# Two mixture stages that gather their expert rows by a list in place of scattering them

## The reference

```python
# first mixture (L0), z = layernorm(x)
gates = softmax(z @ gate_w); topw, topi = top_k(gates, 2); topw /= sum(topw)
h = gelu(_ln(z @ w1[e] + b1[e], ln1_g[e], ln1_b[e])); y[e] = h @ w2[e] + b2[e]
out = _ln(sum over the 2 chosen experts of topw * y[e] + z, ln_g, ln_b)
x = x + out
# second mixture (L2), z = layernorm(x)
v, i = top_k(z @ router_w.T, 2); w = softmax(v)
y[e] = gelu(z @ w1[e].T + b1[e]) @ w2[e].T + b2[e]
x = x + sum over the 2 chosen experts of w * y[e]
```

## Time and profile before

| | |
|---|---|
| median of 3 runs | 2505.26 us (2502.19 to 2505.46) |
| the profiled execution's own time | 2496.09 us |
| its span, first to last instruction | 2494.3 us |
| mean granted TensorE clock | 0.879 |
| PE busy | 1960.8 us (79%) |
| DVE busy | 1378.0 us (55%) |
| ACT busy | 894.4 us (36%) |
| POOL busy | 522.7 us (21%) |

### The profile page before, as it was taken

One profiled execution on the slowest core, in us unless ns is written; L12 is line 12 of the kernel. 1 busy time (PEld: TensorE's weight loads), 2 busy tenths in 40 slices (PEclk: granted clock), 3 DMA queues, 4 the chain that ended last, 5 costly groups with the idle time before them and its releaser, 6 DMA issues. The chain is left out here.

```text
span 2494.3 us, 40430 instructions
## 1 busy us (share of the span) xinstructions
PE 1960.8 (79%) x11858; PEld 1467.3 (59%) x11859; DVE 1378.0 (55%) x3378; ACT 894.4 (36%) x1938; POOL 522.7 (21%) x560
## 2 busy tenths in 40 slices
PE   6997419999800699699979751999999994999587
PEld 4665406666500366366666441899999993565255
DVE  5875426666467477778756443222222222787787
ACT  3452104444311344333312110333333332545587
POOL 1212532211187111101100164000000004562000
PEclk9997559999955799899989655999999996999699
DMA  6000231221121400000000323111111113110001
GB/s 243 1 1 22 80 132 57 63 62 61 56 74 58 180 1 1 13 1 0 0 8 10 135 89 108 30 38 34 38 35 36 38 34 121 39 47 1 8 27 35
DMA packets 81874, 125.70 MB, mean 50 GB/s; under 512 B 17104, under 2 KB 65872, under 8 KB 78704
## 3 DMA queue, kind: packets, MB, share of 16 engines
q1 hardware_dynamic: 46640, 68.02, 8.2%
q0 software_dynamic: 13104, 35.80, 4.4%
q10 hardware_dynamic: 22032, 20.62, 2.4%
HBM read 82.58 MB, written 41.81 MB: 50 GB/s over the span
## 5 line engine op out<-in xcount | busy, mean ns | idle before, releaser
L1386 ACT ACTIVATE e_hT<-psum,e_bt 128x128 f32<-128x128 f32 x568 | 154.2, 383 | 335.3 <-PE psum L1349 335.3
L1349 PEld LDWEIGHTS psum<-e_xT,e_w 128*128 128x128 f32 x2272 | 267.0, 193 | 8.4 <-ACT e_xT L1379 4.9
L1349 PE MATMUL psum<-e_xT,e_w 128*128 128x128 f32 x2272 | 267.7, 276 | 4.2 <-ACT e_xT L1379 4.2
L1358 PE MATMUL psum<-m_w,e_hT 128*128 x1136 | 256.8, 379 | 0.0
L268 POOL TENSOR_TENSOR rstd<-lnt,half 128x4 f32<-128x4 f32 (+1 forms) x72 | 75.6, 1050 | 760.9 <-DVE lnt L262 760.8
L1358 PEld LDWEIGHTS psum<-m_w,e_hT 128*128 128x128 f32 x1136 | 210.4, 190 | 25.7
L1414 DVE COPY e_w<-m_w 128x2048 f32 x71 | 87.1, 1227 | 250.0 <-PE psum L1349 224.6
L698 DVE TENSOR_REDUCE a_mx<-psum 128x8 f32<-128x512 f32 x192 | 123.2, 684 | 109.4 <-PE psum L502 109.1
L483 PE MATMUL psum<-a_cx,att_wk 128*128 128x64 f32 x192 | 29.9, 305 | 165.0 <-DMA a_cx<-in_ctxT 165.0
L1212 ACT ACTIVATE e_hT<-psum,e_bt,e_gt 128x128 f32<-128x128 f32 x284 | 106.7, 456 | 140.8 <-PE psum L1175 140.8
L627 ACT ACTIVATE a_pT<-psum 128x512 f32<-128x512 f32 x192 | 104.0, 594 | 127.3 <-PE psum L552 127.2
(11 more groups left out here) (275 smaller groups left out, 3898.4 us busy)
## 6 DMA issues: line engine op xcount, KB each, us to landing
e_x<-sorted_in SPq DMA_DIRECT2D x142, 128.0 KB, 2.2
sorted_out<-e_y ACTq DMA_DIRECT2D x142, 128.0 KB, 1.7
m_w<-in_L_ffn_w SPq DMA_DIRECT2D x16, 1024.0 KB
m_w<-in_L_ffn_w SPq DMA_DIRECT2D x16, 512.0 KB
x_res<-in_x SPq DMA_DIRECT2D x8, 512.0 KB, 7.1
out_x<-x_res SPq DMA_DIRECT2D x8, 512.0 KB, 2.9
a_cx<-in_ctxT SPq DMA_DIRECT2D x40, 64.0 KB, 2.3
e_b<-in_L_ffn_b SPq DMA_DIRECT2D x2, 1024.0 KB, 4.2
```

What stands on the lines that cost most here:

```text
L1349: mm = pe.matmul(h_b[s][:, f, :], w1[:, kk, f * P:(f + 1) * P], xT[s][:, kk, :], start=(kk == 0), stop=(kk == DC - 1))
L1358: mm = pe.matmul(y_b[s][:, 0:D], hT[s][:, f, :], k.w2[:, bass.ds(e * (FC * D) + f * D, D)], start=(f == 0), stop=(f == FC - 1))
L1386: g = act.activation(hT[s][:, f, :], h_b[s][:, f, :], ACT.Gelu, bias=bt[:, bass.ds(e * FC + f, 1)])
```

## The change

1. **Dispatch.** ACT normalises (with a `shift` per tile) in place of DVE, and SP stores z in token order in a DRAM tensor `rows_in` (512 KB per batch, one store per batch). The selection runs on 16 tiles at once, twice, and all that follows it on all 32 tiles at once. The scatters and zero rows are gone. Instead a list is made for each of the 71 tiles: in 8 chunks of 8 token tiles DVE makes one-hot matrices "row i of a tile" (128 x 1024) and "tile j" (128 x 568) in bf16, POOL and ACT multiply the second by the two halves of the token's number, and PE multiplies the two, which leaves in slot i of tile j the number of its token. `src` is the row to fetch, `dst` the row to send to; unused slots fetch a zero row and send to spare rows. The constants of the experts are loaded by SP in this stage, behind the store of batch 0; for L2 so are the first-layer weights (8 loads of 1 MB), with the stores of batches 1 to 7 behind them. In L2 z has two buffers, so that ACT's batch b waits for the store of batch b-2.
2. **Experts.** SP's loads and ACT's stores are gone. POOL fetches the 128 rows of a tile by an indirect DMA from `rows_in` (`fetch_rows`) and sends y by an indirect DMA to `rows_out`, in the order of tokens (`send_rows`).
3. **Combine.** SP loads the rows of a batch by two plain DMAs of 512 KB. In L0 each of ACT, POOL and DVE works on four tiles; the scaling to unit variance goes from DVE to ACT and the gain from DVE to POOL, the program is written out in full, and there are three buffers. In a3 the fetches leave POOL; those of batches 0 and 1 stand between SP's first loads.

The two DRAM tensors, and in the dispatch SP's stores with the loads behind the first, ACT's `normalise` and DVE's chunks:

```diff
-        self.xs = nc.dram_tensor("sorted_in", [E * CAP + P, D], F32, kind="Internal").ap()
-        self.ys = nc.dram_tensor("sorted_out", [NTILES * P, D], F32, kind="Internal").ap()
+        self.zs = nc.dram_tensor("rows_in", [(1 + NT) * P, D], F32, kind="Internal").ap()
+        self.ys = nc.dram_tensor("rows_out", [(1 + TOPK * NT + NTILES) * P, D], F32, kind="Internal").ap()
...
                 sp.dma_start(gate[:, :, :], k.a[f"L{L}_gate"]).then_inc(w_in, 16)
-                k.late(sp)
+                for b in range(NB):
+                    sp.wait_ge(z_done, b + 1)
+                    sp.dma_start(k.zs[P + b * SEQ:P + (b + 1) * SEQ, :].rearrange("(t p) d -> p t d", p=P),
+                                 z[b % Z].rearrange("p (t d) -> p t d", t=TPB)).then_inc(stored[b % 2], 16)
+                    if b == 0:
+                        k.late(sp)
+                        load_expert_constants(sp, k, L)
...
+                def normalise(b):
+                    wait_pos(act, zT_ps, b - Z + 1)
+                    if b >= Z:
+                        act.wait_ge(stored[b % 2], 16 * (b // 2))
...
+                for c in range(CHUNKS):
+                    s, own = c % 2, slice(c * NJ, (c + 1) * NJ)
+                    wait_pos(dve, ids_ps, c - 1)
+                    dve.tensor_tensor(at_tile[s][:, :, :], k.cst[:, None, C_J:C_J + NTILES].to_broadcast([P, NJ, NTILES]),
+                                      tile_of[:, own, None].to_broadcast([P, NJ, NTILES]), ALU.is_equal).then_inc(hot_done, 1)
+                    dve.tensor_tensor(at_slot[s][:, :, :], k.cst[:, None, C_I:C_I + P].to_broadcast([P, NJ, P]),
+                                      slot[:, own, None].to_broadcast([P, NJ, P]), ALU.is_equal).then_inc(slot_done, 1)
```

The experts of L0 on SP, ACT and POOL:

```diff
-                def step(j, s, first, more):
-                    wait_pos(sp, xT_ps, j - 1)
-                    row = sp.value_load(k.rows[0:1, bass.ds(j, 1)], min_val=0, max_val=E * CAP)
-                    sp.dma_start(xin[s][:, :], k.xs[bass.ds(row, P), :]).then_inc(x_in[s], 16)
...
-                def store(j, s):
-                    act.wait_ge(y_done, j + 1)
-                    act.dma_start(k.ys[bass.ds(j * P, P), :], y[s][:, :]).then_inc(y_out[s], 16)
...
+                for j in range(A + 1):
+                    fetch_rows(pool, k, j, xin, xT_ps)
+                pool.wait_ge(k.const_in, k.consts)
+                for j in range(A):
+                    root(j)
+                for j in range(NTILES):
+                    if j > 0:
+                        send_rows(pool, k, j - 1, y, y_done)
+                    if j + A + 1 < NTILES:
+                        fetch_rows(pool, k, j + A + 1, xin, xT_ps)
+                    if j + A < NTILES:
+                        root(j + A)
+                    if j % 2 and j // 2 < NT // 2:
+                        bias(j // 2)
+                send_rows(pool, k, NTILES - 1, y, y_done)
+                rows_sent(pool, k)
+
+def fetch_rows(pool, k, j, xin, taken):
+    wait_pos(pool, taken, j - 1)
+    pool.indirect_dma_start(
+        out=xin[j % 2][:, :], out_offset=None, in_=k.zs[:, :],
+        in_offset=bass.IndirectOffsetOnAxis(ap=k.src[:, j:j + 1], axis=0)).then_inc(k.row_in[j % 2], 16)
+
+def send_rows(pool, k, j, y, ready):
+    pool.wait_ge(ready, j + 1)
+    pool.indirect_dma_start(
+        out=k.ys[:, :], out_offset=bass.IndirectOffsetOnAxis(ap=k.dst[:, j:j + 1], axis=0),
+        in_=y[j % 2][:, :], in_offset=None).then_inc(k.row_out[j % 2], 16)
```

POOL in the experts of L2, and SP in a3:

```diff
+                for j in range(3):
+                    fetch_rows(pool, k, j, xin, xT_ps)
+                for j in range(NTILES):
+                    if j + 3 < NTILES:
+                        fetch_rows(pool, k, j + 3, xin, xT_ps)
+                    send_rows(pool, k, j, y, y_done)
+                rows_sent(pool, k)
...
+                    if arrival and b < 2:
+                        arrival.fetch(sp, b)
```

More of the change, by code:

```diff
@@ new lines, in dispatch @@
+        zT = [work[:, (2 + s) * DC * SEQ:(3 + s) * DC * SEQ].rearrange("p (c q) -> p c q", c=DC) for s in range(2)]
+        lgt, eq, rest = (sb(nm + n, [P, NT, E]) for n in ("lgt", "eq", "rest"))
+        chosen = k.zero[:, :].rearrange("p (t e) -> p t e", t=NT)
+        ahead, total = [lgt, rest], eq
+        old = {c: k.att_w[c][:, :, :].rearrange("p c d -> p (c d)") for c in "qkvo"}
+        hot, prod = (old[c].rearrange("p (j t e) -> p j t e", j=TOPK, t=NT) for c in "vo")
+        code = sb(nm + "code", [P, NT])
@@ new lines, in select @@
+                        then(dve.tensor_tensor(mine, found, bc(code[:, tiles, None]), ALU.is_equal))
+                        if j == 0:
+                            then(dve.scalar_tensor_tensor(rest[:, tiles, :], mine, -3e38, src, ALU.mult, ALU.add))
+                            src = rest[:, tiles, :]
+                then(dve.scalar_tensor_tensor(shift[:, :], k.mean[:, :], -1.0, k.rstd[:, :], ALU.mult, ALU.mult))
+                dve.sem_inc(centred, 1)
+                for h in range(2):
+                    select(h)
@@ new lines, in _ @@
+                dve.wait_ge(place_ps, 1)
+                for s in range(2):
+                    dve.wait_ge(stored[s], 16 * NB // 2)
+                both = lambda t: t[:, :, :, :].rearrange("p j t e -> p j (t e)")
+                each = lambda t: t[:, :, :, :].rearrange("p j t e -> p (j t) e")
+                tiles = cnt[0]
+                then(dve.tensor_copy(tiles[:, :], pp[:, NT * E:NT * E + E]))
+                then(dve.tensor_tensor(both(prod), both(hot), pp[:, None, 0:NT * E].to_broadcast([P, TOPK, NT * E]), ALU.mult))
@@ L1059, in over_tiles @@
+                then(dve.tensor_tensor(k.dst[:, :], row[:, :], over[:, :], ALU.add))
+CHUNKS, STEPS = 8, 5
 def over_tiles(eng, step, ahead):
@@ L1288, in experts_gelu, with rows_sent @@
+def rows_sent(pool, k):
+    for s in range(2):
+        pool.wait_ge(k.row_out[s], 16 * (k.mixtures + 1) * ((NTILES + 1 - s) // 2))
 def experts_gelu(nc, k):
@@ L1398, in step @@
                         copy(j + 2, s)
[L1399 to L1402 removed]
+                act.wait_ge(k.const_in, k.consts)
                 copy(0, 0)
```

660 lines of the change are left out of this document (282 added, 378 removed).

## The result

| | median of runs | against the kernel before |
|---|---|---|
| before | 2504.11 us (2502.19 to 2505.46) | |
| changed | 2688.51 us (2678.95 to 2691.29) | 1.073 (95% interval 1.0702 to 1.0759) |
| forecast | 2593 us (2520 to 2700) | 1.035 |

A forecast was written before the change was run, and what follows sets the result against it. Both expert stages were taken as PE-bound, the stages between without a full engine. Terms -42 - 27 - 13 - 6 + 230 + 13 - 5 - 51 - 11 = +88 us gave a median of 2593 us, range 2520 to 2700.

The forecast's parts named there:

- The ring: L0 experts: fetch of tile j+3 waits behind send of tile j-1, which waits for y; 7.6 us per tile, +230 us.
- The 0.25 us for DVE's `centre`: L0 ring: time taken for DVE's `centre` holding POOL's issue, chosen between 0 and 0.54 us per tile.
- The bound of 8.2: Upper bound of the L0 ring, in us per tile: full hold and 0.3 us later arrival; +271 us.
- rival (a): L0 experts: PE's clock falls in the ring, making it 9.9 us; +156 us throughout, 2749 us in all; chance 0.2.
- Half the time at the lower clock: Milder case of the falling PE clock in the L0 ring: 2671 us in all.
- Its two rows for and against: Earlier-trace stretches: 0.62 us of work in 3 took the clock from 1.00 to 0.86; 0.17 in 3 kept 1.00.
- Heads and ends: Expert stages: PE starts earlier, -13 us in L0 and -6 in L2; later block ends cost +13 for both.
- Dispatch: Dispatch stages: DVE's chain per batch and the scatters go; -42 us in L0, -27 in L2.
- the wait for the store of batch 1: L2 dispatch: that store queues behind weights and constants on SP, and ACT's batch 3 waits for it; 22 us.
- the -42 named as the lower bound: L2 dispatch: change in us if the stores went around the loads, in place of -27.
- Combine: L0 combine: 143 us becomes 92, at 9.5 us per batch between 7.9 and 11.5; -51 us, bounds -64 and -35.
- a3: a3: plain loads in place of POOL's fetches ahead of the root, -11 us; its late block end lost, -5.

The follow-up runs named there:

- The filled kernel: The changed kernel with 8 more matmuls on PE in each L0 tile, between first layer and transposes: 2614.27 us, 1.0551 times the kernel before.

## Why the prediction was half right

**The ring** was the right mechanism, with the right releaser, place and count: PE waits for fetched rows 69 times (68 forecast), 2.9 us each (2 to 3). Its length at full clock was under-sized, 8.13 us against 7.6, in these links: from the transposes' start to the second layer 0.99 us against 0.60 (the gap behind the transposes is 0.55 us by itself; the 0.60 had taken an overlap from the earlier trace rows where PE did not wait); from the start of y to the send's start 0.71 against 0.57; from the second layer's end to y 0.26 against 0.10; the send 1.08 against 0.96. The arrival was right (1.83 against 1.88). The 0.25 us for DVE's `centre` was too much: only its last 0.17 us lie beside the send, which is 0.1 us longer than a fetch. Together +0.5 us per tile, 68 x 0.5 = 36 us. The bound of 8.2 held.

**The clock** was rival (a), with 0.2, and this is the step that failed: the sum priced the lower clock of the work behind each wait at nothing, and it cost 73 us. Half the time at the lower clock was put at 2671 us; the run gave 2688, with the longer ring. Its two rows for and against the earlier trace rows were single stretches of 3 us out of other stages; the one with PE nearly idle and 1.00 said nothing of a stage in which PE waits 2.9 us in every tile. The likeliest case should have had the clock falling in it: 7.6 + 1.0 in place of 7.6. The filled kernel puts the clock's share at 73 us. The ring's 36 and these 73 are the 110 us of the stage's error.

**Heads and ends.** PE's first matmul in L0 comes 5.7 us into the stage, 11 us earlier than before (13 forecast), in L2 about 4 earlier (6). The ends of both expert blocks cost 7.6 us more than before (13): the 7.9 us from the end of the last scatter's issue to the next block, taken from the earlier trace rows, came to 4.6 in L0 and 5.4 in L2. In L0:

```profile
958.84 0.96 POOL L1277 DMA_INDIRECT rows_out<-e_y,dst  x1 [3.26 <-DVE e_y L1227]
964.36 0.93 SPq L1445 DMA_DIRECT2D c_g<-rows_out  x2
...
1060.16 0.59 POOL L427 MEMSET a_va<- 128x256 f32 x2 [0.90 <-POOLq L226]
```

The last line answers to the earlier trace rows: behind the combine, which no longer has indirect DMAs, POOL starts 0.90 us on in place of 6.12.

**Dispatch.** -52 against -42: a batch takes PE 5.02 us, not 5.4, since transposes and logits overlap by 0.35, and the first 16 logits took 1.91 us, not 3.42; the last logits end 40.0 us into the stage, 7.8 earlier than summed. A chunk takes 2.73 us, between the bounds of 2.0 and 3.4 (3.0 taken), though POOL's product takes 2.05 us and not 1.4. In L2 the wait for the store of batch 1 is there, 23.7 us for 22. The experiment with the loads behind the stores gave 23.5 us back and brought the stage to -53, below the -42 named as the lower bound, by about the 10 us that L0 has too.

**Combine.** -48 against -51, with two errors that cancel. A batch in the middle takes 11.25 us on DVE, near the bound of 11.5, where 9.5 was taken; the first batches and the stage's ends are shorter. What DVE loses there is not in its larger adds, which take 0.48 us (256 elements) and 1.22 us (1024) in these batches:

```profile
1028.81 2.34 POOL L1478 TENSOR_TENSOR x_z<-x_z,c_g 128x1024 f32<-128x1024 f32 x1
...
1029.19 1.99 DVE L254 TENSOR_TENSOR lnt<-stats 128x4 f32<-128x4 f32 x1
1031.10 0.15 DVE L255 TENSOR_TENSOR lnt<-stats 128x4 f32<-128x4 f32 x1
1031.11 2.34 POOL L1482 TENSOR_TENSOR x_z<-x_z,c_g 128x1024 f32<-128x1024 f32 x1
1031.17 2.30 DVE L256 TENSOR_TENSOR mean<-stats 128x4 f32<-128x4 f32 x1
```

Two instructions of four elements, 0.16 us each elsewhere, wait here for POOL's 2.34 us to end. **a3**: -18 against -16.

**Not from the change**: a1 takes 4.8 us more in the profile shown (205.7 against 200.8), with a granted clock of 0.50 in its first 20 us, where it was 0.67 before. In the second profile of the changed kernel it takes 201.2, with 0.65, as in the second of the kernel before (201.2, 0.65). It differs from execution to execution; why is open.

**POOL beside DVE.** In 69 of the 71 tiles the last 0.17 us of `centre` lie beside the send, which takes 1.08 us in the median; in the two last, where nothing lies beside it, it takes 0.96. The send starts 0.29 us behind y's end in both cases. So at most 0.12 us of the ring are its doing, and not 0.54. By the Trainium skill, SBUF — State Buffer, The "DVE blocks DMA" trap, POOL cannot write descriptors while DVE runs a two-port fp32 instruction. The 0.12 us for 0.17 neither show nor refute it; the 0.54 us that the prediction named for it fail because only the end of `centre` falls beside the send. That whichever of DVE and POOL starts first has the shared port pair for its whole instruction (the Trainium skill, SBUF — State Buffer, SBUF: two separate sides) agrees with the combine's rows, 1.99 and 2.30 us for 4 elements; it also fits the chunk's 1.67. By the Trainium skill, DMA: Bandwidth & Descriptors, Anatomy of one DMA, a DMA from POOL takes 2.0 us plus its bytes over 436 GB/s, an estimate of 2.3 us here; 2.8 us was the median of 142 fetches from issue to landing, so the sum was right to go by the row.

## What to carry to other kernels

Where one queue issues a prefetch and also something that waits, write down for each waiting instruction ahead of the prefetch the ring through it, and divide its length by the number of tiles it spans; the pace is about the largest of these and the engines' own (4.42 us was measured where they were 4.06 and 4.22). Removing one ring shows the next, so look for all of them before choosing the order; one more tile of distance, which cost no buffer here, cured nearly all of both. And price a stall of PE twice: once as the wait, and once for the lower clock of the work behind it.

## What was not expected of the hardware

- PE with 3.6 us of useless matmuls in every wait made the stage 73 us shorter: granted clock 1.00 in place of 0.84, second layer 1.99 us in place of up to 3.8.
- A DVE instruction with two inputs and four elements per partition took up to 2.3 us beside a POOL add of 1024 elements, ending when that ended.
- The kernel before takes 2475 to 2504 us, by chip; the changed kernel takes 2689 and 2690 on two of them. No run here tells why.
